# One head's logits a step ahead, four k products first, and k's evacuation ahead of the exponentials in a gated attention block

## The reference

```python
q = rms_norm(layernorm(x) @ q_w ...)          # 16 heads of 128
k = rms_norm(ctx @ ki_w + ki_b); v = ctx @ vi_w + vi_b
scores = einsum('bshd,blhd->bhsl', q, k) / sqrt(128)      # 64 x 64 for each batch and head
attn = softmax(scores); ao = einsum('bhsl,blhd->bshd', attn, v)
x = x + tanh(g_xattn) * (ao @ o_w + o_b)
# then: a mixture of LoRA experts on the normalised x, a second attention over
# 128 x 256 queries, and a feed-forward layer of gated experts, each added to x
```

## Time and profile before

| | us |
|---|---|
| median of 3 runs | 1419.44 (1417.75 to 1420.22) |
| the profiled execution's own time | 1418.54 |
| its span, first to last instruction | 1416.7 |
| TensorE busy in the span | 1283.8 (91%) |
| VectorE busy | 878.7 (62%) |
| ScalarE busy | 802.1 (57%) |
| GpSimd busy | 522.2 (37%) |

### The profile page before, as it was taken

One profiled execution on the slowest core, in us unless ns is written; L12 is line 12 of the kernel. 1 busy time (PEld: TensorE's weight loads), 2 busy tenths in 40 slices (PEclk: granted clock), 3 DMA queues, 4 the chain that ended last, 5 costly groups with the idle time before them and its releaser, 6 DMA issues.

```text
span 1416.7 us, 26442 instructions
## 1 busy us (share of the span) xinstructions
PE 1283.8 (91%) x9889; PEld 1114.4 (79%) x9889; DVE 878.7 (62%) x2164; ACT 802.1 (57%) x2177; POOL 522.2 (37%) x480
## 2 busy tenths in 40 slices
PE   7799998899898998989989899898989999788888
PEld 5578897787788887878779787788877988677777
DVE  3467558764666647666475755756566664676575
ACT  4556776656645565556554666455655556554622
POOL 3685453434333342334333444333443434100000
PEclk8999999999999999999999999999999999989999
DMA  7544354334332334233333334232333242212201
GB/s 284 215 164 159 140 194 164 136 105 142 126 106 80 129 134 149 90 110 112 121 135 110 114 119 147 92 120 91 134 135 119 75 127 97 90 60 75 90 1 46
DMA packets 51693, 171.37 MB, mean 121 GB/s; under 512 B 4592, under 2 KB 23280, under 8 KB 43248
## 3 DMA queue, kind: packets, MB, share of 16 engines
q1 hardware_dynamic: 51568, 169.69, 34.8%
HBM read 148.70 MB, written 20.97 MB: 120 GB/s over the span
## 4 chain that ended last, share of the span: by engine, by line
PE 54%; DVE 26%; ACT 12%; issue 5%; POOL 3%; DMA 0%; SPq 0%; POOLq 0%; ACTq 0%; DVEq 0%
PE bank L116 38%; PE bank L1076 5%; ACT logit L815 4%; ACT xn L851 2%; DVE rstd L82 2%; PE bank L1197 2%; PE bank L1209 2%; DVE ao_lo L1551 2%; PE bank L1087 2%; DVE stats L1586 2%; ACT k_sb L828 2%; PE bank L1065 1%; DVE ntmp L81 1%; ACT ao_hi L809 1%; POOL k_sum L709 1%
## 5 line engine op out<-in xcount | busy, mean ns | idle before, releaser
L703 POOL TENSOR_TENSOR k_sq<-k_sb 128x512 f32<-128x512 f32 x120 | 129.4, 1079 | 369.1 <-ACT k_sb L828 369.1
L713 POOL TENSOR_TENSOR q_sum<-q_sum,q_sq 128x512 f32<-128x512 f32 x120 | 160.0, 1333 | 263.3 <-ACT q_sq L845 262.5
L815 ACT ACTIVATE logit<-logit,least 128x64 f32<-128x64 f32 x512 | 171.2, 338 | 145.7 <-DVE least L1563 145.7
L116 PE MATMUL bank<-xt_hi,wqk 128*128 128x512 f32 x512 | 190.2, 413 | 27.4 <-ACT k_sb L828 22.7
L116 PE MATMUL bank<-ct_hi,wqk 128*128 128x512 f32 x512 | 194.8, 422 | 10.1 <-ACT k_sb L828 4.5
L116 PE MATMUL bank<-so,ao_hi 128*128 128x256 f32 x1008 | 199.7, 296 | 1.5 <-DVE ao_lo L1551 1.3
L116 PE MATMUL bank<-sv,ct_hi 128*128 128x256 f32 x1024 | 198.2, 291 | 0.0
L116 PEld LDWEIGHTS bank<-sv,ct_hi 128*128 128x128 f32 x1024 | 161.3, 192 | 10.1 <-issue 7.7
L1076 PEld LDWEIGHTS bank<-pt,v_sb 128*128 128x128 f32 x1024 | 134.7, 195 | 42.9 <-issue 34.6
L116 PEld LDWEIGHTS bank<-so,ao_hi 128*128 128x128 f32 x1008 | 158.4, 194 | 10.4 <-issue 10.0
L1076 PE MATMUL bank<-pt,v_sb 128*128 128x128 f32 x1024 | 139.6, 280 | 26.4 <-issue 26.4
(11 more groups left out here) (213 smaller groups left out, 2789.5 us busy)
## 6 DMA issues: line engine op xcount, KB each, us to landing
wqk<-qk_scratch SPq DMA_DIRECT2D x56, 1024.0 KB, 5.9
sv<-v_scratch SPq DMA_DIRECT2D x56, 512.0 KB, 3.3
so<-o_scratch SPq DMA_DIRECT2D x56, 512.0 KB, 3.3
qk_scratch<-wqk SPq DMA_DIRECT2D x8, 1024.0 KB, 4.8
xin<-in_x_dram SPq DMA_DIRECT2D x8, 512.0 KB, 7.1
cs<-in_ctx_turned_dram SPq DMA_DIRECT2D x8, 512.0 KB, 7.2
xres<-in_x_dram SPq DMA_DIRECT2D x8, 512.0 KB, 7.9
v_scratch<-sv SPq DMA_DIRECT2D x8, 512.0 KB, 2.6
```

What stands on the lines that cost most here:

```text
L116: last = pe.matmul(out, lhs[a], rhs[b], start=start and n == 0, stop=stop and n == 2, **kw)
L703: pool.tensor_tensor(k_sq[:, h % 2, :] if h else total[0], k_sb[:, h % 2, :], k_sb[:, h % 2, :], ALU.mult).then_inc(k_squared.sem, 1)
L713: pool.tensor_tensor(total[1], total[1], q_sq[:, h % 2, :], ALU.add).then_inc(q_added.sem, 1)
L815: last = act.activation(logit[:, h % 2, t, :], logit[:, h % 2, t, :], ACT.Exp, scale=-1.0, bias=least[:, h % 2, t:t + 1], accum_out=rsum[: ...
```

## The change

In ScalarE's step `project_k` stands ahead of `exps`. In VectorE's step the logits of one head, h-1, are computed in every step, behind share c, and no longer in pairs at the start of even steps; `score_copy` stands behind them, and both are ahead of `prob_copy`. The side work takes its banks in another order, both halves of the transposed x3 and then the norms; `norms` moves from (0, "c") to (0, "d") and `mean_squares` from (0, "c") to (0, "e"). In the prologue four heads' k are projected first (three, the token transposes, the fourth), k_sb has 4 buffers, the weights are split in the order k0, k1, q0, q1, ..., the first context is copied from its input directly, and the first tokens are split half by half straight from PSUM; the warm-up of TensorE is 44 products in place of 24, and for group 0 the adds of q's squares stand on VectorE (`add_first_squares`) in place of GpSimd.

```diff
@@ set-up
-FIRST_K = 2
+FIRST_K = 4
+WEIGHT_ORDER = [(n, p) for p in range(2) for n in ("k", "q")] + [(n, p) for p in range(2, PAIRS) for n in "kq"]
+WEIGHT_ORDER[1], WEIGHT_ORDER[2] = WEIGHT_ORDER[2], WEIGHT_ORDER[1]
-    k_sb = sb("k_sb", [P, 2, GT])
+    k_sb = sb("k_sb", [P, 4, GT])
-    SIDE = [CHOICE[0], ("rk", 0, "F", rk_read), ("rq", 0, "F", rk_read), *CHOICE[1:], *EXPERTS, *MIXTURE,
+    SIDE = [*CHOICE[0:2], ("rk", 0, "F", rk_read), ("rq", 0, "F", rk_read), *CHOICE[2:], *EXPERTS, *MIXTURE,
-        newest[6 + j] = tr_read, 0, j
+        newest[6 + j] = split_lo, 0, 1
@@ SyncE, keep_weights
-            sp.wait_ge(s_wlo, 2 * p + 2)
+            sp.wait_ge(s_wlo, WEIGHT_ORDER.index(("q", p)) + 1)
@@ GpSimd, add_squares
+            if h and g:
                 pool.wait_ge(q_squared.sem, q_squared.count(g, h))
@@ ScalarE
+        def first_context():
+            act.wait_ge(cs_in.sem, cs_in.count(0, 15))
+            for c in range(DC):
+                act.activation(context[0][0][:, c, :], cs[:, c, :], ACT.Copy).then_inc(split_hi.sem, 1)
+
+        def first_tokens(j):
+            act.wait_ge(tr_full.sem, tr_full.count(0, j))
+            act.activation(feature_major(xt_hi, j), token_major(bank_of("tr", j, 0)), ACT.Copy).then_inc(tr_read.sem, 1)
@@ ScalarE, project_k
-            k_squared.wait(act, g, h - 2)
+            k_squared.wait(act, g, h - 4)
@@ ScalarE, step
+            if main and (b >= 0 or h >= FIRST_K):
+                project_k(b + 1, h)
             if live(b, h - TURN_LAG):
                 exps(b, h - TURN_LAG)
-            if main and (b >= 0 or h >= FIRST_K):
-                project_k(b + 1, h)
@@ ScalarE, prologue
-        split_context(0)
+        first_context()
         weight_high("k", 0)
+        weight_high("k", 1)
+        project_k(0, 0)
+        weight_high("q", 0)
         normalise(0)
-        weight_high("q", 0)
-        project_k(0, 0)
         project_k(0, 1)
-        transposed(0, 0)
-        transposed(0, 1)
-        split_tokens(0)
-        weight_high("k", 1)
+        project_k(0, 2)
+        first_tokens(0)
+        first_tokens(1)
+        project_k(0, 3)
         weight_high("q", 1)
@@ TensorE, side work
-            if "F" in parts and at == (0, "c"):
+            if "F" in parts and at == (0, "d"):
                 norms(b)
@@ TensorE, prologue
-        warm(24)
-        for h in range(FIRST_K):
+        warm(44)
+        for h in range(FIRST_K - 1):
             project("k", 0, h)
         for j in range(2):
             transposes(0, j)
+        project("k", 0, FIRST_K - 1)
@@ VectorE, new functions
+        def first_tokens(j):
+            dve.wait_ge(tr_read.sem, tr_read.count(0, j))
+            last = dve.tensor_tensor(feature_major(xt_lo, j), token_major(bank_of("tr", j, 0)),
+                                     feature_major(xt_hi, j).bitcast(F32), ALU.subtract)
+        def add_first_squares(h):
+            dve.wait_ge(q_squared.sem, q_squared.count(0, h))
+            if h > 1:
+                dve.wait_ge(q_added.sem, q_added.count(0, h - 2))
+            dve.tensor_tensor(q_sum[:, 0, :], q_sum[:, 0, :], q_sq[:, h % 2, :], ALU.add).then_inc(q_added.sem, 1)
@@ VectorE, side work
-                if at == (0, "c"):
+                if at == (0, "e"):
                     mean_squares(b)
@@ VectorE, step
-            if h % 2 == 0 and live(b, h - 2):
-                logits(b, h - 2)
-                logits(b, h - 1)
-            if (b, h) == (LAST, H - 1):
-                logits(b, h - 1)
...
+            share(b, h, "b")
+            share(b, h, "c")
+            if live(b, h - 1):
+                logits(b, h - 1)
             if h % 2 == 0 and live(b + 1, h - 2):
                 score_copy(b + 1, h - 2)
-            share(b, h, "b")
-            share(b, h, "c")
+            if b == -1 and h:
+                add_first_squares(h)
             if live(b, h - TURN_LAG):
                 prob_copy(b, h - TURN_LAG)
```

More of the change, by code:

```diff
@@ L702, in add_squares @@
                 k_added.wait(pool, g - 1, H - 2)
-            pool.tensor_tensor(k_sq[:, h % 2, :] if h else total[0], k_sb[:, h % 2, :], k_sb[:, h % 2, :],
+            pool.tensor_tensor(k_sq[:, h % 2, :] if h else total[0], k_sb[:, h % 4, :], k_sb[:, h % 4, :],
                                ALU.mult).then_inc(k_squared.sem, 1)
@@ L826, in project_k @@
             act.wait_ge(k_full.sem, k_full.count(g, h))
-            k_squared.wait(act, g, h - 2)
-            act.activation(k_sb[:, h % 2, :], PRODUCT["k", g, h][0][:, :], ACT.Identity,
+            k_squared.wait(act, g, h - 4)
+            act.activation(k_sb[:, h % 4, :], PRODUCT["k", g, h][0][:, :], ACT.Identity,
                            bias=vecs[:, 3 * H + h:3 * H + h + 1]).then_inc(k_read.sem, 1)
@@ L1087, in scores @@
                     last = pe.matmul(at_ps[i * SEQ:(i + 1) * SEQ, (h % 2 * NT + t) * SEQ:(h % 2 * NT + t + 1) * SEQ],
-                                     q_sb[:, h % 2, s], k_sb[:, h % 2, keys(t, i)], start=True, stop=True)
+                                     q_sb[:, h % 2, s], k_sb[:, h % 4, keys(t, i)], start=True, stop=True)
             if h % 2:
@@ L1136, in project @@
             if g == 0:
-                pe.wait_ge(s_wlo, 2 * p + "kq".index(n) + 1)
+                pe.wait_ge(s_wlo, WEIGHT_ORDER.index((n, p)) + 1)
             else:
@@ L1478, in weight_low @@
         def weight_low(n, p):
-            dve.wait_ge(s_whi, 2 * p + "kq".index(n) + 1)
+            dve.wait_ge(s_whi, WEIGHT_ORDER.index((n, p)) + 1)
             dve.tensor_tensor(weights_of(n, p, 1), raw[n][:, :, pair_columns(p)],
@@ L1533, in score_copy, with first_context @@
                             at_ps[:, :]).then_inc(scores_read.sem, 1)
+        def first_context():
+            dve.wait_ge(split_hi.sem, split_hi.count(0, 1))
+            dve.tensor_tensor(context[0][1][:, :, :], cs[:, :, :], context[0][0][:, :, :].bitcast(F32),
+                              ALU.subtract).then_inc(split_lo.sem, 1)
+        def first_tokens(j):
+            dve.wait_ge(tr_read.sem, tr_read.count(0, j))
+            last = dve.tensor_tensor(feature_major(xt_lo, j), token_major(bank_of("tr", j, 0)),
+                                     feature_major(xt_hi, j).bitcast(F32), ALU.subtract)
+            if j == 1:
+                last.then_inc(split_lo.sem, 1)
+        def add_first_squares(h):
[3 more added lines that the diff above has]
+            dve.tensor_tensor(q_sum[:, 0, :], q_sum[:, 0, :], q_sq[:, h % 2, :], ALU.add).then_inc(q_added.sem, 1)
         def split(g, n):
@@ L1900, in _ @@
         tile_stats(0)
+        first_context()
+        weight_low("k", 0)
         tile_variances()
+        weight_low("k", 1)
         tile_scales()
-        split(0, 0)
-        weight_low("k", 0)
         weight_low("q", 0)
-        split(0, 1)
-        weight_low("k", 1)
+        first_tokens(0)
+        first_tokens(1)
         weight_low("q", 1)
```

## The result

The changed kernel takes 1469.0 us (median of 4 runs, 1458.6 to 1471.4), the kernel before 1419.3: a ratio of 1.034, 95% interval 1.029 to 1.039. It is slower, as forecast, but by 49.7 us and not by 20; the time lies above the range. The profiled execution took 1467.2, with a span of 1465.4.

The account below looks back on a forecast made before the run. TensorE's work plus its waits was taken as the bound; 0 + 10.7 + 5.1 + 10.5 - 6.0 = +20.3 us on a span of 1416.7 led to 1440, own range 1428 to 1449, 8-in-10 range 1408 to 1456.

Parts of the forecast that it names:

- Rest: +1.0 a group: Per group, logits' delay of prob_copy and held probs, less k_sb waits saved: +1.0 us, between -1.7 and +2.2.
- Part 2: Logits one head ahead, after share c: prob_copy delayed, k_sb waits partly gone; +1.0 us a group outside the tail.
- Part 1: Evacuation ahead of exponentials on ScalarE: prob held by GpSimd's k_sum, 0.87 us a bare head; group 0 +10.7, group 1 2.6.
- E: Predicted end of k_sb in a head with nothing beside it, 0.72 us after the k product.
- rival B: TensorE's clock: longer waits at group starts and heads 14, 15 lower it, costing up to 15 us: 1455; chance 0.14.
- Part 3: Norms after the second transposes: norms wait 2.55 us for 1.44, next attention product 2.8; net +1.1 a group, group 1 +1.5.
- Part 4: Tail: logits a head ahead are done in time, so waits for prob shrink; -6.0 us, between 0 and -9.9.
- Part 5: Prologue: time moves into the same transfer wait, some adds go to VectorE; 0 us, between -4.5 and +4.

Follow-up runs that it names:

- The first experiment: The changed kernel with the exponentials ahead of k's evacuation again in ScalarE's step: 1390.1 us, a ratio of 0.979 to the kernel before.

## Why the prediction was wrong

Adding the edits one by one gives a sum that can be laid beside the predicted one: kernel before 1421.6, prologue 1422.4 (+0.8), logits a step ahead 1379.6 (-42.8), later norms 1390.1 (+10.5), swap 1469.0 (+78.9). Predicted were 0 for the prologue, +1.0 a group with -6.0 in the tail for the logits, +7.0 for the norms, and 10.7 and 2.6 for the swap. The total was nearer than its parts, by luck: a gain of 43 was missed, and a loss of 79 was taken for 13 and some shares in the other terms.

Two steps failed, in opposite directions; the second put the time above the range.

**The first step that failed** is "Rest: +1.0 a group" of Part 2, with its reading of who pays for a late logit. I credited the swap with the waits for k_sb and gave the logits' move, the tail left aside, nothing but a delay of prob_copy. The runs show that the move by itself gains 43. The kernel with the logits ahead and the exponentials first, in group 0:

```profile
134.48 0.40 PE L118 MATMUL bank<-ct_hi,wqk 128*128 128x512 f32 x1
134.77 0.34 ACT L827 ACTIVATE logit<-logit,least 128x64 f32<-128x64 f32 x1
...
136.10 0.68 ACT L840 ACTIVATE k_sb<-bank,vecs 128x512 f32<-128x512 f32 x1
136.45 0.42 DVE L1602 TENSOR_TENSOR prob<-logit,rinv 128x256 f32<-128x256 f32 x1
...
139.60 0.38 PE L1078 MATMUL bank<-ident,prob 128*128 128x128 f32 x2
```

The exponentials run while TensorE still makes the k product (it ends at 136.03), so k_sb begins at once behind them and prob misses GpSimd's add, which starts at 137.97. TensorE's waits in this kernel, to be laid beside those of the prologue alone:

```profile
PE bank L118 <- ACT k_sb L840: 11.6, 8, 4.1
...
PE bank L1078 <- DVE prob L1602: 5.7, 5, 1.8
...
PE bank L1061 <- issue: 2.1, 6, 0.4
```

The waits for k_sb fell from 28.1 to 11.6, for prob from 9.9 to 5.7, for the norms from 8.1 to 2.1. I had the sign of this in front of me: the first row has ScalarE waiting 1.86 for `least`, with k_sb behind it in ScalarE's order. ScalarE's waits over the whole kernel before, and in the kernel with the logits ahead:

```profile
ACT logit L815 <- DVE least L1563: 145.7, 48, 6.6
ACT logit L827 <- DVE least L1595: 42.1, 17, 5.2
```

The first experiment's expectation repeats the error: it took the gain for the swap's.

The swap closes the very window that the logits' move opens: alone it costs 38, with the logits ahead 79, as exponentials that stand behind the k product get nothing from early logits.

**The second step that failed** is Part 1's count: "Later groups are full of side work in front of the transposes, which covers 0.9; there it counts in heads 14 and 15 only." The price per bare head was right. Predicted were prob starting at E+1.58, ending 0.28 after the add, transposes 4.43 after the k product and 0.87 lost; measured 1.57, 0.28, 4.42, with a wait of 0.71. But the swap, by the profiled executions with and without it, costs 16.2 in group 0, 9.9 in group 1 and 48.3 in groups 2 to 6 together, where the sum has 10.7, 2.6 and, within the +1.0 of each later group, 1.4 less 0.95, some 2 in the five. Group 2 without the swap, to be laid beside the steady group of the changed kernel:

```profile
405.40:572.40 167.00, 157.06 (x1228) 137.88 (x1227) 104.65 (x266) 98.25 (x268) 64.33 (x58) 0.98 0.36 121
```

At the same clock it is 7.1 shorter, 6.3 of it waits. In each of groups 2 to 6 of the changed kernel the transposes wait for ao_lo four times, 2.7 to 2.8 in all, and not twice; and the late exponentials are paid for a second time, which the sum lacks, at the attention products, whose pt comes late. In group 2 those of heads 12 and 15 wait 2.56 and 4.47, without the swap 0.81 and 1.57. The held prob delays the factor chain at each group's start as well. And 28.1 of the swap's 75.7 are no waits at all but TensorE's busy time, for which the sum has no term (rival B, below).

The reading of the earlier trace rows had a slip: 212.08 lies in group 0, near its end, and not in group 1; the twelve probs at 424 to 429 are those up to 195.4, and of the group's 16 two were already held in the kernel before. It changes no term of the sum.

**Part 3's terms**: the norms' wait 2.52 (predicted 2.55) and the factor chain 4.08 after the k product (586.11 less 582.03, the end of the product's last piece; predicted 4.3) were right. The wait behind them was mis-sized: 4.47 in place of 2.8. It is not at the new group's first attention product, as Part 3 has it, but at that of the old group's head 15, whose pt copy stands behind the new group's first logits. I took 0.5 off for holds that VectorE is spared, where the logits meet the k_sum add of the next head and take 1.53: 1.1 more and not 0.5 less.

**Part 4**: the waits for prob in the tail fell from 9.9 to 5.6, but attention products wait 8.2 there now where they waited 4.6, so the whole stretch from the last group's first attention product to the end became only 1.1 us shorter (171.2 to 170.1), not 6.0. **Part 5** held: 0.8.

**Rival B**, the clock, came on top of the forecast and not in its place. I left the price of the clock out of the sum and gave rival B a chance of 0.14; TensorE's busy time grew by 23.1, and filling one wait a group gave 20 back. A sum of waits that are longer than those before needs a range for the clock behind them.

By the Trainium skill (SBUF — State Buffer, Who interferes with whom) a VectorE instruction with two SBUF inputs and a GpSimd instruction that reads SBUF contend for the ports that they share: the first has them for its whole instruction, and the other fully blocks. The runs agree: prob, started 0.37 into the add, takes 1.21, and with the add cut 0.42; the time falls by 46.

## What to carry to other kernels

Ask of an operation that is moved behind another what the other waits for: exponentials whose input is ready belong in front of an evacuation that waits for the product now running, and the earlier their input, the more this is worth. A chain over several engines should be costed from its first late link to each consumer at every place where it occurs, not at the barest one alone; a change of several edits should be taken apart before it is judged, since here one edit held a gain of 43 and its neighbour a loss of 79. Keep short copies for which TensorE waits ahead of longer work for the next step.

## What the runs showed of the hardware

The clock's price showed more directly than expected. One and the same kernel (the pt copy ahead of the logits) took 1435.1 at a mean clock of 0.982 and 1455.5 at 0.964; and 112 products without use, put into a wait, made a kernel 20 us faster. The number of waits did not decide it: with GpSimd's add cut, the waits for ao_lo fell by 19 us and the mean clock stayed at 0.958, with 41.1 at the attention product, up to 3.9 at once; when those were halved too (19.8), it was 0.982. Nor did their length alone: with the pt copy ahead and the whole add, they were halved as well (27.9) and three of four runs stayed at 0.964, and three groups of one execution of the changed kernel, with the same instructions and the same 16.3 us idle, had clocks of 0.98, 0.96 and 0.95. What else decides it stays open.
